# Moving the transposes and early sums of a pairwise bilinear tower kernel to other places in TensorE's order

## What is computed

```python
e = stack([tbl_f[ids[:, f]] for f in range(32)], axis=1)          # 2048 x 32 x 64
p, q = e[:, row_idx, :], e[:, col_idx, :]                         # triu_indices(32, k=1): 496 pairs
z = einsum('bpe,fpe,bpf->bp', p, kernel, q)                       # 2048 x 496
h = concatenate([z, dense_ctx], axis=1)                           # 2048 x 512
h = maximum(h @ W_top1 + b_top1, 0)                               # 512
h = maximum(h @ W_top2 + b_top2, 0)                               # 256
y = h @ W_top3                                                    # 2048 x 1
```

## Time and profile before

| what | value |
|---|---|
| median of 3 runs | 896.94 us (896.54 to 897.68) |
| profiled execution, its own time | 896.94 us |
| span in the profile | 894.2 us |
| mean granted TensorE clock | 0.989 of full speed |
| PE busy | 831.9 us (93%) |
| DVE busy | 574.1 us (64%) |
| POOL busy | 484.1 us (54%) |
| ACT busy | 114.3 us (13%) |

### The profile page before, as it was taken

One profiled execution on the slowest core, in us unless ns is written; L12 is line 12 of the kernel. 1 busy time (PEld: TensorE's weight loads), 2 busy tenths in 40 slices (PEclk: granted clock), 3 DMA queues, 4 the chain that ended last, 5 costly groups with the idle time before them and its releaser, 6 DMA issues.

```text
span 894.2 us, 10971 instructions
## 1 busy us (share of the span) xinstructions
PE 831.9 (93%) x4496; PEld 293.4 (33%) x4496; DVE 574.1 (64%) x499; ACT 114.3 (13%) x185; POOL 484.1 (54%) x518
## 2 busy tenths in 40 slices
PE   0377999999899999999999999999999999999999
PEld 0122333333333333333333333333333333333323
DVE  0144778778666566787785466787775664788870
ACT  0011010100121011102111110200120210100112
POOL 6777777777777777477735555377746330000000
PEclk9988999999999999999999999999999999999999
DMA  9411111111111111011101111011111000000000
GB/s 340 156 27 26 28 27 27 27 28 27 26 27 26 29 28 26 17 27 26 27 13 21 21 19 22 13 28 25 27 18 22 14 14 1 1 1 1 1 1 0
DMA packets 19881, 27.64 MB, mean 31 GB/s; under 512 B 9012, under 2 KB 9268, under 8 KB 19704
## 3 DMA queue, kind: packets, MB, share of 16 engines
q0 software_dynamic: 16384, 16.81, 10.4%
q1 hardware_dynamic: 3448, 10.14, 3.1%
HBM read 26.91 MB, written 0.01 MB: 30 GB/s over the span
## 4 chain that ended last, share of the span: by engine, by line
PE 69%; POOL 22%; issue 7%; ACT 1%; DMA 0%; DVEq 0%; DVE 0%; ACTq 0%; POOLq 0%
PE y_ps L312 35%; POOL rows L202 22%; PE sum_ps L330 19%; PE side_ps L250 5%; PE side_ps L238 3%; PE side_ps L257 2%; PE y_ps L315 1%; PE y_ps L273 1%; ACT xt L363 1%; PE y_ps L283 1%; PE y_ps L313 1%; PE side_ps L264 1%; PE y_ps L278 0%; DMA rows<-tbl_dram,idx 0%; DMA idx<-ids_dram 0%
## 5 line engine op out<-in xcount | busy, mean ns | idle before, releaser
L461 DVE TENSOR_TENSOR products<-y_ps,xt 128x1024 f32<-128x1024 f32 x480 | 556.3, 1217 | 287.2 <-PE y_ps L313 287.0
L202 POOL DMA_INDIRECT rows<-tbl_dram,idx x512 | 483.4, 944 | 239.7 <-issue 151.7
L312 PE MATMUL y_ps<-xt,kernel_sb 64*128 64x512 f32 x960 | 459.0, 616 | 4.1 <-ACT xt L363 4.1
L313 PE MATMUL y_ps<-xt,kernel_sb 64*128 64x512 f32 x960 | 459.2, 617 | 0.0
L312 PEld LDWEIGHTS y_ps<-xt,kernel_sb 64*128 64x128 f32 x960 | 168.6, 190 | 256.7 <-issue 145.0
L330 PE MATMUL sum_ps<-products,selector 128*32 128x512 f32 x1984 | 238.8, 598 | 0.7 <-DVE products L461 0.7
L313 PEld LDWEIGHTS y_ps<-xt,kernel_sb 64*128 64x128 f32 x960 | 168.6, 190 | 0.0
L330 PEld LDWEIGHTS sum_ps<-products,selector 128*32 128x32 f32 x1984 | 51.6, 109 | 170.4 <-DVE products L461 94.2
L363 ACT ACTIVATE xt<-side_ps 128x512 f32<-128x512 f32 x64 | 38.2, 598 | 442.9 <-PE side_ps L238 442.8
L238 PE MATMUL side_ps<-identity,rows 128*128 128x128 f32 x256 | 44.2, 298 | 46.1 <-DMA rows<-tbl_dram,idx 46.1
L238 PEld LDWEIGHTS side_ps<-identity,rows 128*128 128x128 f32 x256 | 28.3, 146 | 100.2 <-issue 60.1
(11 more groups left out here) (29 smaller groups left out, 73.1 us busy)
## 6 DMA issues: line engine op xcount, KB each, us to landing
rows<-tbl_dram,idx POOLq DMA_INDIRECT x512, 2.4
kernel_sb<-pair_kernel_dram SPq DMA_DIRECT2D x15, 512.0 KB, 11.1
w_sb<-w_dram SPq DMA_DIRECT2D x1, 1024.0 KB, 18.2
w_sb<-w_dram SPq DMA_DIRECT2D x1, 512.0 KB, 17.5
kernel_sb<-pair_kernel_dram SPq DMA_DIRECT2D x1, 256.0 KB, 2.8
z_sb<-dense_dram SPq DMA_DIRECT2D x16, 8.0 KB
idx<-ids_dram SPq DMA_DIRECT2D x1, 192.0 KB, 6.9
idx<-ids_dram SPq DMA_DIRECT2D x1, 64.0 KB, 1.9
```

Source lines behind the costliest of these rows:

```text
L202: pool.indirect_dma_start(rows[:, slot, t, h, :], None, tables[j], bass.IndirectOffsetOnAxis(ap=idx[:, c, t, j:j + 1], axis=0)).then_inc(r ...
L312: nc.tensor.matmul(y[:, 0, :], kernel_sb[low, d, :], x_of(c, q)[low, :], start=True, stop=True)
L313: last = nc.tensor.matmul(y[:, 1, :], kernel_sb[high, d, :], x_of(c, q)[high, :], start=True, stop=True)
L461: nc.vector.tensor_tensor(products[:, g % PRODUCT_RING], y_ps[g % Y_RING][:], by, ALU.mult).then_inc(duo_multiplied, 1)
```

## The change

The side jobs get other places. In chunk 0, q1 to q7 stand right in front of FIRST_DUO[q]; q8 and later go in front of the last duo with d % 4 == 2 that is at least 2 duos ahead of FIRST_DUO[q] (at least 4 in the other chunks), and at least four duos ahead of the following transpose. The layers take the free ones of the places d % 4 == 2, so that no place has two side jobs. The new places:

- chunk 0: q7 at d22, q8, q9, q10 at d26, 34, 42, q11 to q15 at d54, 66, 78, 90, 106, the next chunk's q0 to q3 at d110, 114, 118, 122 (q0 to q6 of chunk 0 as before).
- chunk 1 (2 and 3 alike): q4, q5, q6 at d2, 6, 10, q7 to q10 at d18, 26, 34, 42, q11 at d50, q12 at d62, q13, q14, q15 at d74, 90, 102, the next chunk's q0 to q3 at d110 to d122; layer1 blocks at d14, 22, 30, 38, layer2 blocks at d54, 58, layer3 at d70.

In chunk 0, up to d21, sums are also made after the duo in front of a transpose (after d0, d2, d6, d10, d15, d21): all quads whose two duos have been issued. After d15 and d21 that includes the duo just issued.

`special_slots(c, u)` now follows the `store` of pair 4u + 3 in every chunk. `z_sb` has a fifth bank, and a chunk's four banks rotate through the five; ACT's wait for the previous chunk's layer1 moves from a chunk's first bank to its second.

```diff
+Z_RING = 5
-def quads_after(d):
-    return (d // 2 - 2, d // 2 - 1) if d % 4 == 1 else ()
-
-def after_sums(d):
-    return d - (d - 2) % 4
+def sum_schedule():
+    after, summed = {}, 0
+    waits = [FIRST_DUO[q] - 1 for q in range(2, 8)]
+    for c in range(CHUNKS):
+        for d in range(DUOS):
+            if c == 0 and d in waits:
+                upto = (d + 1) // 2
+            elif d % 4 == 1:
+                upto = c * QUADS + d // 2
+            else:
+                upto = summed
+            after[c, d] = [divmod(quad, QUADS) for quad in range(summed, upto)]
+            summed = max(summed, upto)
+    return after
+
+SUMS_AFTER = sum_schedule()
 def side_schedule():
     before = {(c, d): [] for c in range(CHUNKS) for d in range(DUOS)}
     for c in range(CHUNKS):
-        for q in range(PAIRS):
-            if c == 0:
-                at = 0 if q < 2 else FIRST_DUO[q] if q < 7 else after_sums(min(FIRST_DUO[q] - 4, 30 + 6 * (q - 8)))
-                before[0, at].append(("turn", 0, q))
-            elif q < 8:
-                before[c - 1, after_sums(82 + 6 * q if c == 1 else 66 + 7 * q)].append(("turn", c, q))
+        later = CHUNKS * DUOS
+        for q in reversed(range(PAIRS)):
+            if c == 0 and q < 8:
+                at = FIRST_DUO[q] if q else 0
             else:
-                before[c, after_sums(6 + 7 * (q - 8))].append(("turn", c, q))
+                at = c * DUOS + FIRST_DUO[max(q, 1)] - (2 if c == 0 else 4)
+                at = later = min(at - (at - 2) % 4, later - 4)
+            before[divmod(at, DUOS)].insert(0, ("turn", c, q))
     for c in range(CHUNKS - 1):
+        free = [d for d in range(6, DUOS, 4) if not before[c + 1, d]]
         for n in range(4):
-            before[c + 1, after_sums(10 + 6 * n)].append(("layer1", c, n))
+            before[c + 1, free[n]].append(("layer1", c, n))
         for n in range(2):
-            before[c + 1, after_sums(38 + 8 * n)].append(("layer2", c, n))
-        before[c + 1, after_sums(60)].append(("layer3", c, 0))
+            before[c + 1, free[5 + n]].append(("layer2", c, n))
+        before[c + 1, free[8]].append(("layer3", c, 0))
...
+        def z_of(c, kb):
+            return z_sb[:, (c * Z_BANKS + kb) % Z_RING]
...
                     bilinear(c, d)
-                    for quad in quads_after(d):
-                        if quad >= 0:
-                            add_up(c, quad)
-                        elif c:
-                            add_up(c - 1, QUADS + quad)
+                    for of, quad in SUMS_AFTER[c, d]:
+                        add_up(of, quad)
...
-                if c and kb == 0:
+                if c and kb == 1:
                     act.wait_ge(side_ready, SIDE["layer1", c - 1, 3] + 1)
...
                         keep(job)
-                        if c == 0 and job[0] == "turn" and job[1] == 0 and job[2] % 4 == 3:
-                            special_slots(0, job[2] // 4)
-                    for u in range(SPECIALS):
-                        if c and d == max(0, SPECIAL_DUO[u] - 14):
-                            special_slots(c, u)
+                        if job[0] == "turn" and job[2] % 4 == 3:
+                            special_slots(job[1], job[2] // 4)
```

More of the change, by code:

```diff
@@ L132, in dlrm_tower @@
         products = sb("products", [P, PRODUCT_RING, 2, N])
-        z_sb = sb("z_sb", [P, Z_BANKS, N])
+        z_sb = sb("z_sb", [P, Z_RING, N])
         w1_sb = sb("w1_sb", [P, 4, H1])
@@ L217, in place_dense @@
                 for g in range(4):
-                    sp.dma_start(z_sb[32 * g + SUM_ROWS:32 * g + 32, LAST_BANK, :],
+                    sp.dma_start(z_of(c, LAST_BANK)[32 * g + SUM_ROWS:32 * g + 32, :],
                                  dense[4 * g:4 * g + 4, c * N:c * N + N]).then_inc(dense_landed[c], 16)
@@ L249, in layer1 @@
                 for kb in range(4):
-                    last = nc.tensor.matmul(tower_bank(c, 1, n), w1_sb[:, kb, n * P:n * P + P], z_sb[:, kb, :],
+                    last = nc.tensor.matmul(tower_bank(c, 1, n), w1_sb[:, kb, n * P:n * P + P], z_of(c, kb),
                                             start=(kb == 0), stop=(kb == 3))
@@ L272, in last_tower @@
                     for kb in range(LAST_BANK):
-                        nc.tensor.matmul(tower_bank(c, 1, n), w1_sb[:, kb, n * P:n * P + P], z_sb[:, kb, :],
+                        nc.tensor.matmul(tower_bank(c, 1, n), w1_sb[:, kb, n * P:n * P + P], z_of(c, kb),
                                          start=(kb == 0), stop=False)
@@ L277, in last_tower @@
                 for n in range(4):
-                    nc.tensor.matmul(tower_bank(c, 1, n), w1_sb[:, LAST_BANK, n * P:n * P + P], z_sb[:, LAST_BANK, :],
+                    nc.tensor.matmul(tower_bank(c, 1, n), w1_sb[:, LAST_BANK, n * P:n * P + P], z_of(c, LAST_BANK),
                                      start=False, stop=True).then_inc(side_ready, 1)
@@ L415, in copy_bank @@
                 act.wait_ge(quad_summed, c * QUADS + min(Z_QUADS * (kb + 1), QUADS))
-                if c and kb == 0:
+                if c and kb == 1:
                     act.wait_ge(side_ready, SIDE["layer1", c - 1, 3] + 1)
                 if kb < LAST_BANK:
-                    copy(z_sb[:, kb, :], sum_ps[:]).then_inc(bank_kept, 1)
+                    copy(z_of(c, kb), sum_ps[:]).then_inc(bank_kept, 1)
                 else:
@@ L422, in copy_bank @@
                         part = slice(32 * g, 32 * g + SUM_ROWS)
-                        copy(z_sb[part, kb, :], sum_ps[part, :]).then_inc(bank_kept, 1)
+                        copy(z_of(c, kb)[part, :], sum_ps[part, :]).then_inc(bank_kept, 1)
             for c in range(CHUNKS):
@@ L428, in _ @@
                         keep(job)
-                        if c == 0 and job[0] == "turn" and job[1] == 0 and job[2] % 4 == 3:
-                            special_slots(0, job[2] // 4)
-                    for u in range(SPECIALS):
-                        if c and d == max(0, SPECIAL_DUO[u] - 14):
-                            special_slots(c, u)
[L434 to L438, removed]
+                        if job[0] == "turn" and job[2] % 4 == 3:
+                            special_slots(job[1], job[2] // 4)
+                    for of, quad in SUMS_AFTER[c, d]:
+                        if quad % Z_QUADS == Z_QUADS - 1 or quad == QUADS - 1:
+                            copy_bank(of, quad // Z_QUADS)
             copy_bank(CHUNKS - 1, LAST_BANK)
```

## The result

The changed kernel takes 875.47 us (median of 4 runs, 875.41 to 875.53) against 897.01 us (4 runs): a ratio of 0.9759, 95% interval 0.9742 to 0.9776. The forecast was 876.6 us. The profiled execution takes 875.41 us with a span of 873.6 us; 873.9 was forecast.

A forecast was written before the change was run, and what follows sets the result against it. PE's fixed order of work was taken as the bound, with gathers limiting the start-up. Span 894.2 - 3.2 - 7.1 - 10.0 = 873.9 us, with 2.7 around it 876.6 us; own range 875 to 878.

The forecast's parts named there:

- (a): Chunk 0's start-up: PE reaches q8's transpose when its rows arrive, 94.2 instead of 97.41 us, saving 3.2 us.
- (b): Gather waits behind 97 us go: 5.35 us idle plus 1.7 us of low clock, together 7.1 us.
- modelled ends of the sums: Ahead of each gather wait behind 97 us: up to 0.3 us more gain than the 7.1.
- low-clock stretch: Behind the 1.92 us gather wait, clock 0.72: four duos take 5.33 us instead of 3.64, 1.7 us more.
- q6's margin: Chunk 1, fourth transpose in the densest run: rows are there in time by 0.4 us or more.
- (c): Layer blocks in chunks 1 to 3 no longer wait for ACT's copy behind a transpose: 10.0 us saved.
- (d): Remaining changes (last bank's copy, fifth z_sb bank, dense rows' placing, q15's store in chunk 0) cost nothing.
- R1: Flush or thin margin costs: q8 late or q6 of chunk 1 waits; 1.7 to 4.5 us less gained; chance 0.18.
- R2: The 10.0 us from separating layers and transposes return as waits for DVE: 886.6 us; chance 0.07.
- R3: Gather waits move instead of going, since the ring holds POOL; 7.1 us stay, 883.7 us; chance 0.06.
- DVE's margin: Each group of four duos: DVE needs 4.9 us against PE's 5.49, 0.6 us margin even without waits.
- R4: Gathers between chunks become the bound, slower than before; 900 us if a pair takes 3 us over 10; chance 0.03.

The follow-up runs named there:

- f4: Changed kernel with chunk 0's q8 at d28 and q9 at d36, each two duos later: 875.12 us, ratio 0.9745.
- f1: Changed kernel with the layer blocks put behind transposes again in four places of a chunk: 885.42 us, ratio 0.9858.
- e7: Changed kernel with chunk 0's q8 at d28 and q9 at d36, on a chip with late signals: 1057.62 us, ratio 0.9497.
- e2: Changed kernel with layer blocks behind transposes again in four places of a chunk, on a chip with late signals: 1084.22 us, ratio 0.9572.
- e5: Changed kernel with three slots of gathered rows instead of four, on a chip with late signals: 1049.16 us, ratio 0.9398.
- e6: Changed kernel with two slots of gathered rows instead of four, on a chip with late signals: 1035.7 us, ratio 0.928.

## Why the prediction was right

The forecast was 1.1 us high, and the result is within its own range of 875 to 878. By its steps:

(a) 3.2 us forecast, 97.41 - 94.14 = 3.27 us in the trace. The way there was put 1.3 us too long in all (93.6 against 92.3), nearly all of it ahead of q6, and what hid it was the wait at the end. q6 was put at 76.9 us and came at 75.73, since PE got its full clock sooner in this execution; from q6 to q7 10.5 us were measured and 10.7 forecast, from q7 to the point of q8 6.1 and 6.0; in f4, with the lower clock for longer, d26 came at 93.45 where 93.6 was forecast for the same point. The bound ahead was the arrival of the rows, 94.2, and it held to 0.1 us.

(b) 7.1 us forecast, with up to 0.3 more for the modelled ends of the sums. Parts (a) and (b) in f1 are 10.6 us of span, less the arrival at q8 there (97.41 - 94.24 = 3.2): 7.4 us. The four waits are gone, and with them the low-clock stretch of the earlier trace rows: the clock is 1.00 in every window behind 80 us. POOL restarted 0.93 us after q15's transpose and its 32 gathers ran at 1.249 us each as worked out; q6's margin was 0.95 us where at least 0.4 was forecast; PE took 43.09 us for the seven steps instead of 42.56, since the two steps with a special duo took 6.44 and 6.24 us instead of 6.08. The reading from the trace stands; the price if that margin is overrun was not measured.

(c) 10.0 us forecast, 9.95 us measured by f1 and 3.3 us a chunk in the traces. Counting from the start of the transpose to the start of the layer block was worth 0.7 us over the idle notes alone.

(d) Nothing was seen of a cost: PE has no wait behind q8 but one of 0.67 us in front of the last sums, which the kernel before has too.

Sum of the measured terms: 3.3 + 7.4 + 10.0 = 20.7 us; the spans differ by 894.2 - 873.6 = 20.6. So the sum over the span missed by 0.3 us, and most of the forecast's miss of 1.1 us is outside the span: 875.41 - 873.6 = 1.8 us where 2.7 was carried over from one profiled execution. In the comparisons f1 and f4 the runs of the kernel before have 1.8 to 3.0 us around their spans, so one run was a poor measure of this term.

The rivals. R1 (878 to 881 us) did not come, and f4 shows how near it was: with a start-up made 1.1 to 1.2 us later by the low clock PE still had 0.7 us to spare at q8, not more. R2 is refuted by f1. R3 by the trace: POOL was held for 12.86 us in one piece and PE ran on. DVE's margin was enough in every group. The Trainium skill (Perfetto Trace Analysis, section Identifying the Most-Contended Engine) judges TensorE's headroom by its share of peak work (MFU) or by the busy share of weight loads, and the prediction argued against going by the latter. That share is 33% in both kernels, yet the 17.7 us of idle time that were closed all came off the span; here the unbroken order on the engine was the better sign. R4 did not come; in this trace nothing stretched the gathers (each still 0.94 us long, 1.249 apart), with DVE busy 15.19 of 20 us.

## What to carry to other kernels

Where one engine runs in a fixed order without a pause, find its last forced wait (here the arrival of one field pair) and add the durations of what stands behind it; a reordering can take away the waits behind that point and what hangs on them. Here these were 5.35 and 9.3 us of idle time, some 2.7 us that the low clock and the steps around the waits cost over it, and 3.3 us by which PE reached the point itself too late. Two jobs that share one buffer want a job of the other kind between them longer than the copy that frees it; 12 places at 0.83 us were half of the gain here. A job that needs a transfer stands better near its own first use than as early as there is a place, if the rate of the transfers and the release of their slots, worked through at the densest run, leave the rows in time there; here they did by 0.95 us. A small wait in front of a late transfer can be what absorbs the variation of the start-up, so filling it may give less than its length (0.35 of 1.82 us in f4).

## What the runs showed of the chip that I had not expected

The same program took 897 to 899 us in three comparisons and 1115 to 1139 us in four others on other chips, with instructions of the same length and late starts behind other engines. Ratios changed with it: the kernel with q8 and q9 later has 0.9745 in f4 and 0.9497 in e7, the one with the layers behind 0.9858 in f1 and 0.9572 in e2. So a comparison of a few us stands only where the kernel before takes its usual time.

In the three traces of one such chip (e7, e5, e6) the first late copy by ACT started 7 to 9 us after POOL's last gather into a free slot had begun: at 80.74 us with four slots, 70.29 with three, 59.17 with two.

The granted clock in the start-up differs between executions of the same order: 0.56 against 0.72 in 64 to 70 us, worth 1.1 us at d26. And an idle time of 1.82 us in front of q8 was not followed by a lower clock (1.00), while one of 1.92 us in the kernel before was (0.72).
